# Ties at a row's threshold: kept by counting in the sorted list, instead of equality passes and a scan

## The chip, the cores and the metric

One core of a Trainium2 chip. The metric is device time in microseconds of one execution of the whole kernel, as the median of several runs. TensorE does the matmuls and transposes, VectorE and ScalarE the work on elements, GpSimd small powers; DMAs are issued by SyncE's queue (SP).

## The reference, cut to what matters

Four graph layers follow each other on `x` [2048, 128] with an adjacency of 2048 x 2048. The second one contains two attention steps with top-p sparsification, and the change lies there:

```python
probs = softmax(q @ k.T)                       # [2048, 2048]
idx = argsort(-probs)
sp = take_along_axis(probs, idx); cs = cumsum(sp)
keep_sorted = cs - sp < 0.9                    # TOP_P
mask = zeros.at[rows, idx].set(keep_sorted)
A = probs * mask
A = A / max(A.sum(-1), 1e-12);  Xa = A @ Xa    # twice, STEPS = 2
```

Per row the largest probabilities are kept until their sum reaches 0.9. The cut falls between two neighbours of the sorted row. If those two are equal (a tie), a comparison with the smallest kept value keeps both, and one of the equals has to be dropped: argsort is stable, so the first ones in the row are kept.

## The kernel before, in words

The 2048 rows are 16 tiles of 128. An attention step goes over four groups of four tiles (`G = 4`), so there are eight calls of `group(E, gi, left)`: `gi` 0 to 3 in the first step, 4 to 7 in the second; `left` counts the groups that still follow in the step (3 down to 0). `E` holds four tiles of unnormalised probabilities, 128 x 2048 float32 each, in `EA` for even and `EB` for odd groups.

VectorE works off its own instruction stream in program order. In a group it does the following.

1. `third_sum` and the steps before it guess a threshold `q.th` for each row, just above the true one.
2. `under` (L1934) writes the values under the guess into `cands[k]`; eight maxima of 8 values each per tile (L2071), then rounds of maximum and `match_replace` on 64 values (L2081, L2085) make `L`, the 32 largest values under the guess in sorted order. `crossing_checked` (L1954) scans `L` with the missing mass, adds 4.0 to the values behind the cut and takes the minimum: `s_(0)`, that is `s4[:, 0, :]`, the smallest kept value, a row's threshold. `after` is the largest value not kept.
3. `doubtful` (L2020) sets flags in `fl`: column 0 if anything is odd in any row, column `UNSURE` (4) if the list didn't reach the cut, columns `TIE + k` (8 to 11) if tile k has a row with `after >= s_(0)`. `any_row` (L1721) turns the 32 x 32 blocks of `fl` and reduces them, so that column 1 of `fl` holds each flag once for each block of 32 partitions.
4. With `left > 0`, first sums of the next group follow and the maximum of the one after next. `load_more()` (L1726) then loads flag 0 into four registers, one for each partition block, and adds them. With `left > 0` the masks are issued ahead of the branch: `masked` (L1967) writes `E * (E >= threshold)` to `cands[k]` with its sum in `Sk`.
5. `dve.If(more[0])`: the branch for odd groups. With `left == 0` it makes the masks there. It loads `UNSURE`; if that is set, `surely` (L2000) brackets and searches anew. Then `cut` (L1981) checks each tile's flag with `load_more(TIE + k)`, and for a tile with ties does an equality pass, a 2048-wide scan for the running sum of the tied values, three small steps, and two passes that subtract the surplus ones.
6. With `left == 0` the masks are made behind the branch (L2118 to L2121), each releasing TensorE by `mask_ok`; otherwise `kept_ok` (L2126, the reciprocal `rS`) releases it for the whole group.

`Steps` and `Dyn` count every VectorE instruction on a semaphore: `w(ins)` issues and waits for it, `w.put(ins)` only issues. `Dyn` counts from a register's value, for use inside branches, and `end` asserts its number of steps.

TensorE's order is written out by hand. `attend` (L746 on) transposes the kept rows (L527) and multiplies them (L778). For the last group of the second step (`gi == 7`) it comes behind `multiplied(3)` to `multiplied(11)` (L847), products of the third layer whose operands ScalarE finishes in L1267 and L1320. SP loads natural tiles of `adj` into `EA` behind `kept_ok` of group 6 and into `EB` behind that of group 7.

Of the kernel before, what the change touches and what calls it, by code (L numbers as in the profile page):

```python
# [7 lines left out]
ALU = mybir.AluOpType  # L8
# [6 lines left out]
P = 128  # L15
# [24 lines left out]
TOP = 8  # L40
# [54 lines left out]
def gnn_kernel(nc, x, adj, W0, b0, W1, W2, W3, U1, U2, ln_g, ln_b, L2W, L3W, b3, out):  # L95
# [18 lines left out]
    with ExitStack() as ctx:  # L114
        def sb(name, shape, dt=F32):
            return ctx.enter_context(nc.sbuf_tensor(name, shape, dt))
# [84 lines left out]
        fl = sb("fl", [P, 32], I32)  # L201
        ft = sb("ft", [P, 32], I32)
        ones = sb("ones", [P, WINDOW])
        Sk = sb("Sk", [P, G])
        rS = sb("rS", [P, 2, G])

# [1266 lines left out]
        def _(dve):  # L1473
# [3 lines left out]
            def tt(o, x0, x1, op):  # L1477
                return dve.tensor_tensor(o, x0, x1, op)
# [8 lines left out]
            def total(o, x0, op=ALU.add):  # L1487
                return dve.tensor_reduce(o, x0, AX.X, op)
# [17 lines left out]
            v.put(dve.memset(ones[:, :], 1.0))  # L1506
            v.put(dve.memset(below[:, :, :], 0.0))
            v(dve.memset(fl[:, :], 0))
            dve.wait_ge(in_x, 16)
            dve.wait_ge(expo_ok, 2)  # L1510
            sq_early = XT[:, BK:2 * BK].rearrange("p (k c) -> p k c", c=P)
# [214 lines left out]
            def load_more(c=0):  # L1726

                for m in range(4):
                    dve.reg_load(more[m], fl[32 * m + c:32 * m + c + 1, 1:2])
                for m in range(1, 4):  # L1730
                    dve.reg_add(more[0], more[0], more[m])

            def unfinished(w, window):

# [232 lines left out]
            def masked(w, E):  # L1967

                for k in range(G):
                    w.put(stt(cands[k], E[:, k, :], s4[:, 0, k:k + 1], ALU.is_ge, E[:, k, :], ALU.mult,  # L1970
                              accum_out=Sk[:, k:k + 1]))
# [9 lines left out]
            def cut(E, Tt, last):  # L1981


                for k in range(G):
                    load_more(TIE + k)
                    with dve.If(dve.snap(more[0])):
                        c = Dyn(sure_steps, sures, 8)
                        c(stt(tied, E[:, k, :], s4[:, 0, k:k + 1], ALU.is_equal, E[:, k, :], ALU.mult,
                              accum_out=Fv[:, k:k + 1]))
                        whole, spare = (E[:, k, :], cands[k]) if last else (cands[k], E[:, k, :])  # L1990
                        c.put(dve.tensor_tensor_scan(spare, tied, tied, 0.0, ALU.add, ALU.max))
                        c(tt(s4[:, 2, k:k + 1], Sk[:, k:k + 1], Tt[:, k:k + 1], ALU.subtract))
                        c(tt(s4[:, 2, k:k + 1], s4[:, 2, k:k + 1], Fv[:, k:k + 1], ALU.subtract))
                        c(tt(s4[:, 3, k:k + 1], s4[:, 0, k:k + 1], s4[:, 2, k:k + 1], ALU.subtract))
                        c(stt(tied, spare, s4[:, 3, k:k + 1], ALU.is_ge, tied, ALU.mult))
                        c(stt(whole, tied, -1.0, ALU.mult, whole, ALU.add, accum_out=Sk[:, k:k + 1]))
                        c.settle()
                        c.end()

            def surely(w, E, gi):  # L2000


                bracket(w, gi)
                unfinished(w, TOP)
                w.settle()
                more_rounds(E, gi, TOP)
                for k in range(G):
                    under(w, E, hi, k)
                w.wait()
                w.settle()  # L2010
                for k in range(G):
                    w.put(dve.max(V[:, k, :], cands[k]))
                w.wait()
                crossing(w, V, CU, TOP)
                masked(w, E)
                w.wait()
                ties(w)
                any_row(w)
# [15 lines left out]
            def group(E, gi, left):  # L2034


                q = guess_of[gi % 2]
                nq = guess_of[1 - gi % 2]

                def next_max(k):  # L2040
                    if left > 0:
                        row_max(gi + 1, k, k % 2)

                if gi in BOTH:
                    def early():
                        logit_mean(gi + 1)
                        next_max(0)

                    first_sums(E, gi, early)
                    third_sum(E, gi, lambda: next_max(1))  # L2050
                else:
                    third_sum(E, gi, lambda: next_max(1))

                for k in range(G):
                    if gi > 0:

                        dve.wait_ge(e_turned, 4 * (G * (gi - 1) + k + 1))
                    if gi not in BOTH and k == 0:
                        next_max(2)
                    under(v, E, q.th, k, accum_out=Lw[:, k:k + 1])  # L2060
                    v.wait()
                    if gi not in BOTH and k == 1:
                        next_max(3)
                    if k == G - 1:
                        v.put(tt(q.fval, q.spare, Lw[:, :], ALU.subtract))
                    for s in range(SETS):
                        if s == SETS // 2 and k < 2 and gi in BOTH:
                            next_max(k + 2)
                        if s == SETS // 2 and k == 2 and left > 0:
                            guess_gap(gi + 1)  # L2070
                        v.put(dve.max(tops[0][:, k, s * TOP:(s + 1) * TOP], cands[k][:, s * N // SETS:(s + 1) * N // SETS]))  # L2071
                    if k == 2 and left > 0:
                        guess_first(gi + 1)
                        dve.sem_inc(th_ok, 1)
                v.wait()
                v.put(total(seen8, tops[0][:, :, TOP - 1:SETS * TOP:TOP], ALU.max))
                for m in range(WINDOW // TOP):
                    if m > 0:

                        for k in range(G):  # L2080
                            v.put(dve.match_replace(tops[m % 2][:, k, :], L[:, k, (m - 1) * TOP:m * TOP],  # L2081
                                                    tops[(m - 1) % 2][:, k, :], 0.0))
                        v.wait()
                    for k in range(G):
                        v.put(dve.max(L[:, k, m * TOP:(m + 1) * TOP], tops[m % 2][:, k, :]))  # L2085
                    v.wait()
                if left > 1:
                    logit_mean(gi + 2)
                crossing_checked(q)
                doubtful()  # L2090
                if left > 0:
                    last_tile(nq, gi + 1)
                    surplus_below(nq, gi + 1, 0)
                    last_surplus(nq)
                    first_step(nq)
                    dve.sem_inc(th_ok, 1)
                    remember(nq, 0)
                if left > 1:
                    row_max(gi + 2, 0)
                load_more()  # L2100
                if left > 0:
                    masked(v, E)
                with dve.If(dve.snap(more[0])):
                    if left > 0:
                        v.wait()
                    else:
                        m = Dyn(sure_steps, sures, G)
                        masked(m, E)
                        m.wait()
                        m.end()  # L2110
                    load_more(UNSURE)
                    with dve.If(dve.snap(more[0])):
                        w = Dyn(sure_steps, sures, 52)
                        surely(w, E, gi)
                        w.settle()
                        w.end()
                    cut(E, q.Tt, left == 0)
                if left == 0:  # L2118
                    for k in range(G):
                        stt(cands[k], E[:, k, :], s4[:, 0, k:k + 1], ALU.is_ge, E[:, k, :], ALU.mult,  # L2120
                            accum_out=Sk[:, k:k + 1]).then_inc(mask_ok, 1)  # L2121
                    dve.wait_ge(mask_ok, G * (gi // NB + 1))
                else:
                    v.wait()
                v(ts(Sk[:, :], Sk[:, :], 1e-12, ALU.max))
                dve.reciprocal(rS[:, gi % 2, :], Sk[:, :]).then_inc(kept_ok, 1)  # L2126
                if left > 0:
                    v(tt(pa, soft, nq.inv_slope, ALU.mult))
                    v(tt(num, num, pa, ALU.add))
                    last_tile(nq, gi + 1)  # L2130
                    surplus_below(nq, gi + 1, 1)
                    last_surplus(nq)
                    next_step(nq, 0)
# [294 lines left out]
```

## Time and profile before

| | |
|---|---|
| median of 3 runs | 1088.53 us |
| lowest to highest | 1083.34 to 1089.64 us |
| the profiled execution: time | 1088.74 us |
| its span, first to last instruction | 1087.0 us |
| its mean granted TensorE clock | 0.854 of full |
| busy: PE, DVE, ACT, POOL | 75%, 75%, 47%, 6% |

The span is what the rows below count in; the 1.7 us between it and the execution's own time lie around it. PE is TensorE, DVE VectorE, ACT ScalarE, POOL GpSimd. A line such as L1485 is that of a helper (`stt`), so many different steps carry it; names and shapes tell them apart. An idle stretch "<-issue" is time in which the engine waited for nothing that the trace shows: its sequencer was busy with register loads, branches or fetching.

### The profile page before, as it was taken

The page shows a single profiled execution, that of the slowest core. Times are in us where ns is not written, and L with a number is a line of the kernel's source. Part 1 is how long each engine was busy: PE and PEld are TensorE (multiplying, and loading weights), DVE is VectorE, ACT ScalarE, POOL GpSimd, SP SyncE. Part 2 cuts the span into 40 slices and gives each one's busy share as a digit, 9 for nine tenths or more (in the row PEclk, how much of TensorE's full clock was granted, in tenths as well). Part 3 has the DMA queues.
Part 4 walks back from the last instruction along what each step waited for, and adds up shares of the span by engine and source line. Part 5 has one row for each costly group of instructions (what it writes and reads, how often), then busy time and mean ns, then how long its engine had stood idle before and what let it go on. Part 6 is the DMA issues. An engine that isn't in the chain of part 4 may idle for free. (4 is left out here: it accounts for less than half of the span.)

```text
span 1087.0 us, 12342 instructions
## 1 busy us (share of the span) xinstructions
PE 810.0 (75%) x3871; PEld 561.4 (52%) x3871; DVE 811.3 (75%) x2389; ACT 505.8 (47%) x973; POOL 70.5 (6%) x63
## 2 busy tenths in 40 slices
PE   5879968877886827376788787686088869997695
PEld 5744425555765717274565576573085456543342
DVE  5977769898999989933989898997789463235715
ACT  4867235366567475134526656748334122123212
POOL 0020000000000000000000000101001101002201
PEclk9989957888988868789796899898588989998798
DMA  9859203424013000000242402303141337600001
GB/s 342 337 190 432 75 9 146 150 83 156 1 45 112 1 2 1 0 2 0 78 155 82 151 1 75 135 1 126 39 163 39 117 120 296 281 1 0 1 0 39
DMA packets 20222, 108.25 MB, mean 100 GB/s; under 512 B 1825, under 2 KB 8753, under 8 KB 9777
## 3 DMA queue, kind: packets, MB, share of 16 engines
q1 hardware_dynamic: 18752, 106.77, 26.5%
q10 hardware_dynamic: 1392, 0.61, 0.2%
q8 instruction: 29, 0.48, 0.2%
q14 instruction: 49, 0.39, 0.1%
HBM read 88.23 MB, written 19.14 MB: 99 GB/s over the span
## 5 line engine op out<-in xcount | busy, mean ns | idle before, releaser
L1049 ACT ACTIVATE AT<-PS 128x512 f32<-128x512 f32 (+2 forms) x240 | 118.8, 553 | 167.3 <-PE PS L527 137.0
L527 PE MATMUL PS<-ident,AT 128*128 128x128 f32 x544 | 88.3, 300 | 110.2 <-DVE rS L2126 66.4
L527 PEld LDWEIGHTS PS<-ident,AT 128*128 128x128 f32 x544 | 70.8, 155 | 118.4 <-DVE rS L2126 69.0
L1485 DVE SCALAR_TENSOR_TENSOR AT<-EA,se 128x2048 uint8<-128x2048 f32 (+1 forms) x46 | 107.6, 2346 | 2.0 <-PE PS L527 0.7
L700 PE MATMUL PS<-K,ST 64*128 64x512 f32 x256 | 90.3, 802 | 22.6 <-ACT EA L1182 12.4
L1485 DVE SCALAR_TENSOR_TENSOR AT<-AT 128x2048 uint8<-128x2048 f32 (+2 forms) x50 | 100.7, 2013 | 1.1
L2071 DVE MAX8 AT<-AT 128x8 f32<-128x256 f32 x256 | 87.6, 412 | 0.7
L1624 DVE TENSOR_REDUCE mxv<-PS 128x1 f32<-128x2048 f32 x32 | 73.2, 2288 | 15.8 <-PE PS L700 15.4
L778 PE MATMUL PS<-hr,AT 128*128 128x128 f32 x512 | 71.7, 290 | 8.7 <-ACT AT L1049 7.8
L778 PE MATMUL PS<-AT 128*128 128x128 f32 x512 | 71.9, 290 | 7.7 <-ACT AT L1049 7.1
L778 PEld LDWEIGHTS PS<-hr,AT 128*128 128x128 f32 x512 | 65.2, 200 | 17.9 <-ACT AT L1049 11.9
L778 PEld LDWEIGHTS PS<-AT 128*128 128x128 f32 x512 | 65.4, 201 | 16.4 <-ACT AT L1049 11.8
L592 PE MATMUL PS<-AT 128*128 128x256 f32 x256 | 65.7, 415 | 10.5 <-DVE gs L1482 8.9
L592 PE MATMUL PS<-AT,hr 128*128 128x256 f32 x256 | 64.3, 408 | 11.8 <-DVE gs L1482 10.7
L1485 DVE SCALAR_TENSOR_TENSOR AT<-AT,s 128x2048 f32<-128x2048 f32 x22 | 50.6, 2349 | 24.5 <-issue 24.3
L592 PEld LDWEIGHTS PS<-AT 128*128 128x128 f32 x256 | 52.1, 209 | 25.2 <-DVE gs L1482 12.8
L592 PEld LDWEIGHTS PS<-AT,hr 128*128 128x128 f32 x256 | 51.1, 206 | 25.7 <-DVE gs L1482 14.2
L1049 ACT ACTIVATE ST<-PS 128x512 f32<-128x512 f32 (+2 forms) x35 | 19.2, 555 | 91.0 <-PE PS L1003 22.8
L700 PEld LDWEIGHTS PS<-K,ST 64*128 64x128 f32 x256 | 30.8, 240 | 57.4 <-issue 50.3
L651 PE MATMUL PS<-AT,R 128*128 128x512 f32 x128 | 58.4, 611 | 0.0
L1003 PE MATMUL PS<-AT,R 128*128 128x512 f32 x128 | 57.2, 592 | 0.0
L847 PE MATMUL PS<-AT,hr 128*128 128x512 f32 x96 | 48.7, 662 | 11.1 <-ACT hr L1320 11.1
(297 smaller groups left out, 1462.8 us busy)
## 6 DMA issues: line engine op xcount, KB each, us to landing
AT<-keep_at SPq DMA_DIRECT2D x32, 1024.0 KB, 5.1
EA<-in_adj SPq DMA_DIRECT2D x20, 1024.0 KB, 6.8
keep_at<-AT SPq DMA_DIRECT2D x8, 2048.0 KB, 24.9
AT<-keep_at SPq DMA_DIRECT2D x8, 2048.0 KB, 14.4
AT<-in_adj SPq DMA_DIRECT2D x12, 1024.0 KB, 4.9
EA<-keep_degrees SPq DMA_DIRECT2D x1, 1024.0 KB, 6.4
keep_x<-K SPq DMA_DIRECT2D x4, 256.0 KB, 6.9
out<-EA SPq DMA_DIRECT2D x4, 256.0 KB, 2.3
```

Source lines behind the costliest of these rows:

```text
L527: return pe.transpose(dst, src, ident[0:p, 0:p])
L592: mm = pe.matmul(bank(6)[:, 2 * P:4 * P], left[:, j, :], slab[:, j, :], start=(j == 0), stop=(j == NT - 1))
L651: mm = pe.matmul(halves(4 + b % 2), R[:, j, :], AT[:, 2 * b:2 * b + 2, j, :], start=(j == 0), stop=(j == NT - 1))
L700: return pe.matmul(bank(to + n), ST[1][half_rows, k * P:(k + 1) * P], keys[half_rows, n * BK:(n + 1) * BK], start=True, stop=True)
L778: mm = pe.matmul(bank(6)[:, 0:P], stg[b % 2][:, n * P:(n + 1) * P], left[:, j, :], start=(j == 0), stop=(j == NT - 1))
L847: mm = pe.matmul(bank(n), hr[:, t, :], natural(t)[:, n * BK:(n + 1) * BK], start=(t == 0), stop=(t == NT - 1))
L1003: mm = pe.matmul(halves(4 + i % 2), R[:, j, :], AT[:, 2 * b:2 * b + 2, j, :], start=(j == 0), stop=(j == NT - 1))
L1049: return act.activation(dst, src, ACT.Copy)
L1485: return dve.scalar_tensor_tensor(out=o, in0=x0, scalar=s, in1=x1, op0=op0, op1=op1, **k)
L1624: v(dve.tensor_reduce(mxv[:, odd:odd + 1], PS[:, b:b + 4, :], AX.XY, ALU.max))
L2071: v.put(dve.max(tops[0][:, k, s * TOP:(s + 1) * TOP], cands[k][:, s * N // SETS:(s + 1) * N // SETS]))
```

## The change

A row of counts 1 to 8 (`counted`) is made once at the start. In the branch, `tied_counted` counts for each row how often the threshold occurs among the kept values of the sorted list `L`, and makes `V`: the threshold that many times, then zeros. More than 8 occurrences make the row unsure. `joined` brings each flag of the four partition blocks into one, so that a flag is one register load (`load_joined`) in place of four and three adds. For a tile with ties `first_tied` lets `match_replace` put 4.0 in the place of the first occurrences of the values in `V`, and one pass keeps what is greater than the threshold. With `left == 0` the masks inside the branch are gone. `surely` and `cut` stay for unsure groups; `first_tied` stands in the Else part.

```diff
--- before.py
+++ after.py
@@ -201,6 +201,8 @@
         fl = sb("fl", [P, 32], I32)
         ft = sb("ft", [P, 32], I32)
         ones = sb("ones", [P, WINDOW])
+        counted = sb("counted", [P, TOP])
+        flags = sb("flags", [P, 4], I32)
         Sk = sb("Sk", [P, G])
         rS = sb("rS", [P, 2, G])
 
@@ -1506,6 +1508,7 @@
             v.put(dve.memset(ones[:, :], 1.0))
             v.put(dve.memset(below[:, :, :], 0.0))
             v(dve.memset(fl[:, :], 0))
+            v(dve.tensor_tensor_scan(counted[:, :], ones[:, 0:TOP], ones[:, 0:TOP], 0.0, ALU.mult, ALU.add))
             dve.wait_ge(in_x, 16)
             dve.wait_ge(expo_ok, 2)
             sq_early = XT[:, BK:2 * BK].rearrange("p (k c) -> p k c", c=P)
@@ -1729,6 +1732,17 @@
                     dve.reg_load(more[m], fl[32 * m + c:32 * m + c + 1, 1:2])
                 for m in range(1, 4):
                     dve.reg_add(more[0], more[0], more[m])
+
+            def joined(w):
+
+                for m in range(4):
+                    w.put(dve.tensor_copy(flags[0:32, m:m + 1], fl[32 * m:32 * (m + 1), 1:2]))
+                w.wait()
+                w(dve.tensor_reduce(ft[0:32, 0:1], flags[0:32, :], AX.X, ALU.max))
+
+            def load_joined(c):
+
+                dve.reg_load(more[0], ft[c:c + 1, 0:1])
 
             def unfinished(w, window):
 
@@ -1994,6 +2008,31 @@
                         c(tt(s4[:, 3, k:k + 1], s4[:, 0, k:k + 1], s4[:, 2, k:k + 1], ALU.subtract))
                         c(stt(tied, spare, s4[:, 3, k:k + 1], ALU.is_ge, tied, ALU.mult))
                         c(stt(whole, tied, -1.0, ALU.mult, whole, ALU.add, accum_out=Sk[:, k:k + 1]))
+                        c.settle()
+                        c.end()
+
+            def tied_counted(w):
+
+                w(tt(LS[:, :, :], L[:, :, :], s4[:, 0, :].unsqueeze(2).to_broadcast([P, G, WINDOW]), ALU.is_equal))
+                w(total(s_(2), LS[:, :, :]))
+                w.put(tt(V[:, :, :], counted[:, :].unsqueeze(1).to_broadcast([P, G, TOP]),
+                         s4[:, 2, :].unsqueeze(2).to_broadcast([P, G, TOP]), ALU.is_le))
+                w(ts(s_(5), s_(2), TOP + 0.5, ALU.is_gt))
+                w.put(tt(V[:, :, :], V[:, :, :], s4[:, 0, :].unsqueeze(2).to_broadcast([P, G, TOP]), ALU.mult))
+                w(tt(s_(5), s_(5), s_(3), ALU.max))
+                w(dve.tensor_reduce(fl[:, UNSURE:UNSURE + 1], s_(5), AX.X, ALU.max))
+                any_row(w)
+                joined(w)
+
+            def first_tied(E, last):
+
+                for k in range(G):
+                    load_joined(TIE + k)
+                    with dve.If(dve.snap(more[0])):
+                        c = Dyn(sure_steps, sures, 3)
+                        c(dve.match_replace(tied, V[:, k, :], E[:, k, :], 4.0))
+                        c(stt(E[:, k, :] if last else cands[k], tied, s4[:, 0, k:k + 1], ALU.is_gt, E[:, k, :], ALU.mult,
+                              accum_out=Sk[:, k:k + 1]))
                         c.settle()
                         c.end()
 
@@ -2103,18 +2142,18 @@
                 with dve.If(dve.snap(more[0])):
                     if left > 0:
                         v.wait()
-                    else:
-                        m = Dyn(sure_steps, sures, G)
-                        masked(m, E)
-                        m.wait()
-                        m.end()
-                    load_more(UNSURE)
+                    t = Dyn(sure_steps, sures, 14)
+                    tied_counted(t)
+                    t.end()
+                    load_joined(UNSURE)
                     with dve.If(dve.snap(more[0])):
                         w = Dyn(sure_steps, sures, 52)
                         surely(w, E, gi)
                         w.settle()
                         w.end()
-                    cut(E, q.Tt, left == 0)
+                        cut(E, q.Tt, left == 0)
+                    with dve.Else():
+                        first_tied(E, left == 0)
                 if left == 0:
                     for k in range(G):
                         stt(cands[k], E[:, k, :], s4[:, 0, k:k + 1], ALU.is_ge, E[:, k, :], ALU.mult,
```

## Rows read from the trace of the kernel before

**Rows 1.** Page, part 1: busy us of each engine (share), instructions

```profile
PE 810.0 (75%) x3871; PEld 561.4 (52%) x3871; DVE 811.3 (75%) x2389; ACT 505.8 (47%) x973; POOL 70.5 (6%) x63
```

**Rows 2.** VectorE's timeline in group 6: start us, us, what, [idle before, releaser]

```profile
759.40 2.35 DVE L1485 SCALAR_TENSOR_TENSOR AT<-EA,s 128x2048 f32<-128x2048 f32 x1 [1.73 <-issue]
...
773.22 2.35 DVE L1485 SCALAR_TENSOR_TENSOR AT<-EA,s 128x2048 f32<-128x2048 f32 x1 [4.64 <-issue]
...
775.61 4.42 DVE L1991 TENSOR_TENSOR_SCAN EA<-AT 128x2048 f32<-128x2048 f32 x1
...
792.18 0.17 DVE L1482 TENSOR_SCALAR Sk<-Sk 128x4 f32<-128x4 f32 x1 [6.99 <-issue]
```

**Rows 3.** VectorE's timeline in group 7

```profile
842.75 2.35 DVE L1485 SCALAR_TENSOR_TENSOR AT<-AT,s 128x2048 f32<-128x2048 f32 x1 [2.15 <-issue]
...
865.62 2.35 DVE L1485 SCALAR_TENSOR_TENSOR AT<-AT,s 128x2048 f32<-128x2048 f32 x1 [13.70 <-issue]
...
868.01 4.42 DVE L1991 TENSOR_TENSOR_SCAN AT<-AT 128x2048 f32<-128x2048 f32 x1
...
877.74 2.35 DVE L1485 SCALAR_TENSOR_TENSOR AT<-AT,s 128x2048 f32<-128x2048 f32 x1
```

**Rows 4.** TensorE's waits, 740 to 890: us in total, times, longest

```profile
PE PS L527 <- DVE rS L2126: 32.6, 1, 32.6
...
PE PS L527 <- DVE AT L1485: 9.6, 1, 9.6
```

**Rows 5.** TensorE's timeline, 792 to 896

```profile
792.62 1.97 PE L527 MATMUL PS<-ident,AT 128*128 128x128 f32 x8 [32.64 <-DVE rS L2126]
...
854.88 12.20 PE L847 MATMUL PS<-EA,hr 128*128 128x512 f32 x24 [3.16 <-ACT hr L1320]
866.92 3.60 PE L847 MATMUL PS<-AT,hr 128*128 128x512 f32 x8
880.15 1.97 PE L527 MATMUL PS<-ident,AT 128*128 128x128 f32 x8 [9.64 <-DVE AT L1485]
...
889.14 0.27 PE L527 MATMUL PS<-ident,T 128*128 128x128 f32 x1
...
895.70 0.27 PE L527 MATMUL PS<-ident,T 128*128 128x128 f32 x1
```

**Rows 6.** VectorE's small steps before the branch of group 6

```profile
746.61 0.29 DVE L1478 TENSOR_TENSOR AT<-AT 128x124 f32<-128x124 f32 x1
...
748.84 0.16 DVE L2031 TENSOR_REDUCE fl<-s 128x1 int32<-128x4 f32 x1
749.03 0.21 DVE L1723 STREAM_TRANSPOSE ft<-fl 128x32 int32<-128x32 int32 x1
749.28 0.19 DVE L1724 TENSOR_REDUCE fl<-ft 128x1 int32<-128x32 int32 x1
```

**Rows 7.** VectorE's timeline in group 3, branch not taken

```profile
465.89 2.35 DVE L1485 SCALAR_TENSOR_TENSOR AT<-AT,s 128x2048 f32<-128x2048 f32 x1 [4.84 <-issue]
```

**Rows 8.** VectorE by line and shape: count, busy us, mean ns, idle before

```profile
L2071 DVE MAX8 AT<-AT 128x8 f32<-128x256 f32 x256 | 87.6, 412 | 0.7
...
L2085 DVE MAX8 AT<-AT 128x8 f32<-128x64 f32 x128 | 19.3, 213 | 0.8
L2081 DVE MATCH_REPLACE8 AT<-AT 128x64 f32<-128x64 f32 x96 | 19.0, 209 | 0.0
...
L2081 DVE MATCH_VALUE_LOAD AT<-AT 128x8 f32 x96 | 8.1, 84 | 0.8
```

**Rows 9.** Stretches: length, busy us of PE, PEld, DVE, ACT, POOL, clock, DMA share, GB/s

```profile
880.00:889.00 9.00, 8.85 (x55) 8.61 (x56) 7.89 (x11) 2.85 (x6) 0.00 (x0) 0.69 0.12 15
889.00:896.00 7.00, 6.83 (x59) 6.35 (x57) 0.00 (x0) 3.62 (x10) 0.00 (x0) 1.00 0.97 404
```

**Rows 10.** VectorE at the start

```profile
11.49 2.29 DVE L1488 TENSOR_REDUCE nd<-EA 128x1 f32<-128x2048 f32 x1 [10.44 <-DMA K<-in_x]
```

## The prediction

> **What bounds the kernel now.** I read the page's busy shares first [rows 1]. TensorE and VectorE are each busy three quarters of the span, so no engine's total settles anything. What counts is who waits at the place the diff touches. The diff works inside one branch of `group`, so the second view is VectorE's timeline, to see in which of the eight groups (two steps of four) that branch runs. The 2048-wide scan of line 1991 stands there twice, in groups 6 and 7 counting from 0 [rows 2, 3]. No instruction of lines 2007 to 2018 (`surely`) is in the trace. So the branch runs in the last two groups, each time for ties in one tile, and the expensive search never. The reader should see there the three passes over 2048 values and, larger, the holes marked "issue": VectorE idles 4.64 and 6.99 us around group 6's tie pass and 13.70 us before group 7's [rows 2, 3]. In them its sequencer loads flags into registers and branches.
>
> Third, TensorE's waits between 740 and 890 us [rows 4]: 32.6 us for `rS`, the last thing group 6 makes, and 9.6 us for a row mask of group 7. So both tails release TensorE. TensorE's timeline [rows 5] gives the important detail. After group 6 is released at 792.62 it has its own work until 870.52 (the last batch starts at 866.92 and lasts 3.60), and only then waits, until 880.15. What group 7 saves beyond those 9.64 us relative to TensorE is worth nothing.
>
> **What goes, what comes.** In group 6 the tail runs from the end of the masks, 773.22 - 4.64 = 768.58, to 792.18: 23.60 us. It is 4.64 idle, 11.97 of passes and small steps (773.22 to 785.19), 6.99 idle [rows 2]. The last hole is three checks of later tiles that turn out false, 2.33 each; the first is two checks, 2.32 each. Each check is four register loads, three adds, a branch and the skip. The four loads and adds alone, ahead of the masks, leave a hole of 1.73 [rows 2], so branch and skip are 0.60.
>
> The new tail, added up:
> - `tied_counted`, 14 steps: two over 128 values at 0.29 plus some 0.03 between [rows 6]; transpose and reduction of the flags 0.45; the others small, 0.19 apart when they wait [rows 6], about 0.1 when they don't. 0.64 + 0.45 + five waited at 0.2 + two put and four copies at 0.08 to 0.1 = 2.6 us; 3.0 if the copies between partition blocks hold each other up.
> - Five checks with one load in place of four. If the four loads share 1.73 evenly, one is 0.43 and a check 1.03. If the 1.73 is one latency that four overlapping loads share, a check stays at 2.33. Neither row decides; I take 0.7 for the load, nearer to the even share because the adds also belong to the 1.73, so 1.3 a check, 6.5 us.
> - The way to the Else part skips `surely` and all four bodies of `cut`. For a long skip the trace has two answers: group 3, whose branch is not taken, leaves 4.84 us before its masks, group 7, whose branch is taken, 2.15 [rows 3, 7], so the skip of the whole body costs 2.69; while skipping `surely` alone in group 6 costs no more than a short one (two checks in 4.64). The new skip is nearly the whole body: I take 2.7, bound 0.
> - The tie pass of one tile: value load 0.08, replacement over 2048, product 2.35. Replacement is seen only over 64 values, 209 ns; the maximum instruction gives a slope, (412 - 213) / 192 = 1.04 ns a value [rows 8], so 209 + 1984 x 1.04 = 2.27 us; upper bound the scan's 4.42 [rows 2]. With gaps 4.8 us, bound 7.0. I take the slope: both instructions cost the same at 64.
>
> Sum 2.6 + 6.5 + 2.7 + 4.8 = 16.6 us against 23.60: group 6 saves 7.0 us (bounds: 12.6 new, saves 11.0; 24.4 new, loses 0.8). TensorE starts right behind `rS` [rows 5], and its work up to 870.52 hangs on it, directly or through ScalarE and GpSimd steps that it feeds, so I move all of it by the full saving. The natural tiles that SP loads when group 6 reports (and, later, those of group 7) are issued earlier by as much. VectorE's group 7 moves as well; it has no hole before 842.75 but the 2.15 of its loads and branch.
>
> In group 7 the tail runs from 842.75 to 877.74, where the final masks start: 34.99 us [rows 3]. It holds four masks whose result only `cut` used; they go to the unsure branch, where they don't run. The new tail is again 16.6, so the masks come 18.4 us earlier; even at the upper bound of 24.4 they come 10.6 earlier. Either way TensorE's wait of 9.64 goes entirely, and what is late next is TensorE's own work before it. Group 7 gives 9.6 us, whatever the unknown prices.
>
> A second gain follows. After the wait TensorE's granted clock is at the low level: 0.69 of full in 880 to 889, 1.00 in 889 to 896 [rows 9]. The first tile takes 880.15 to 889.14 = 8.99 us, the second, with no less work, 6.56 [rows 5]. Without the idle stretch the last batch before it, and so the first tile too, run at 2.4 GHz: 2.4 us more.
>
> Costed at nothing: the scan of `ones` into `counted` lies in VectorE's wait of 10.44 us for the first input [rows 10]; were it exposed it would be some 0.2 us. In the six groups without ties the branch only skips a longer body; in five of them behind four masks of 2.3 us each, as today, and in group 3 exposed, with 2.7 us already paid. The new waits are all VectorE on its own steps; behind them stand the final masks and `rS`, for which TensorE waits, and they are in the 2.6.
>
> **Two rules of the Trainium skill beside the rows.** The Trainium skill, DMA: Bandwidth & Descriptors (Latency and other measured facts), gives a register load a floor of about 600 ns and says that the compiler unrolls four of them to spread it. That speaks against this change, which replaces four loads by a lone one: an estimate by that page is 1.2 us a check and a gain of 19.5 in all; no run here shows one load alone. Its page Runtime: NRT & Kernel Launch (Instruction fetch mechanics) says that a taken branch to outside the fetched window stalls for a fetch. Group 3 agrees (4.84 against 2.15), group 6's skip does not show it; by the rule the skip costs its 2.7, without it the whole gain would be 21.7.
>
> **The sum.** 7.0 + 9.6 + 2.4 = 19.0 us. The profiled execution took 1088.74, span 1087.0; the median is 0.2 below, so 1088.53 - 19.0 = 1069.5. The three runs spread over 6 us, and about 1% is what a measurement of this kernel can tell from no change.
>
> **The rivals.**
> - Checks cost by latency, not by count: 2.33 each, so group 6 saves 7.0 - 5.2 = 1.8, or loses 0.8 if replacement also goes at the scan's rate. With 12.0 from group 7 the gain is 11 to 14 us: 1074.5 to 1077.5. For it: nothing in the trace separates the loads. Chance 0.20.
> - Everything cheap: checks 1.03, no stall at the skip. Group 6 saves 11, together 23: 1065.5. Chance 0.08.
> - Group 7's gain is lost: some other input of TensorE's work after 870.52 is late, or its earlier work doesn't move with the release. Only group 6's 7 us stay: 1081.5. Against it: TensorE's waits between 740 and 890 that name a step of another engine name steps fed by TensorE itself, but for these two. Chance 0.07.
> - Slower: the count makes rows unsure that were not. It decides when some row holds nine or more kept values equal to its threshold (above TOP + 0.5). Then `surely` runs: four `under` passes and four masks and four tie passes at 2.35, four 2048-wide maxima at 412 + 1792 x 1.04 = 2.27 us, together 37 us, and some 10 of loads, checks and small steps, without a single round of search; `cut` stays on top. One group so hit gives about 1135, two 1180. For it only that a threshold of many equal values is conceivable; against it, only one tile of each group has ties. This is also the case that the change doesn't do what it says. Chance 0.05.
> - The forecast, gain 16 to 22 with the tie pass or a check off by a little: 0.60.
>
> 1064 to 1078 takes in the forecast, both cases of the check's price and their bounds, and leaves out the last two rivals, 0.12, and some spread. Faster by over 1% (10.9 us): forecast, the cheap case and nearly all of the first rival, 0.85. Within 1%: its edge and the lost gain, 0.10. Slower 0.05.
>
> **What the new profile would show.** No scan on 2048 values, a replacement of about 2.3 us in groups 6 and 7; holes of about 1.3 us per check in place of 2.33 (the first rival says 2.3); one hole of some 4 us before the tie pass; no wait of TensorE between its last batch and the first transposes of group 7, and that tile in 6.6 us at full clock; TensorE's wait for group 6's `rS` about 7 us shorter. Wrong would be: any instruction of `surely`, TensorE waiting for something new ahead of group 7, or a replacement near 4 us.

## The result, and the profile after

| | before | after |
|---|---|---|
| median | 1088.76 us (4 runs, 1083.34 to 1089.64) | 1060.60 us (4 runs, 1059.20 to 1062.30) |
| profiled execution, span | 1088.74, 1087.0 us | 1062.30, 1060.5 us |

The ratio is 0.9756, with a 95% interval from 0.9726 to 0.9785: some 26.6 us faster (23 to 30) where 19.0 was forecast, and below the range, which ended at 1064. A second measurement on another chip gave 0.9757 (0.9732 to 0.9783). The two profiled executions differ by 26.5 us in span; that is the difference to account for.

VectorE's timeline in group 6 of the changed kernel answers to [rows 2] (helpers have moved by two lines):

```profile
758.53 2.35 DVE L1487 SCALAR_TENSOR_TENSOR AT<-EA,s 128x2048 f32<-128x2048 f32 x1 [1.75 <-issue]
...
767.83 0.29 DVE L1480 TENSOR_TENSOR AT<-AT,s 128x128 f32<-128x128 f32 x1
...
770.43 0.14 DVE L1741 TENSOR_REDUCE ft<-flags 32x1 int32<-32x4 int32 x1
774.70 0.09 DVE L2033 MATCH_VALUE_LOAD AT<-AT,EA 128x8 f32 x1 [4.12 <-issue]
774.78 2.28 DVE L2033 MATCH_REPLACE8 AT<-AT,EA 128x2048 f32<-128x2048 f32 x1
777.09 2.35 DVE L1487 SCALAR_TENSOR_TENSOR AT<-AT,s,EA 128x2048 f32<-128x2048 f32 x1
...
781.90 0.17 DVE L1484 TENSOR_SCALAR Sk<-Sk 128x4 f32<-128x4 f32 x1 [2.45 <-issue]
```

The masks end at 767.71. Counting, flags and joining take 2.86 us to 770.57. Then come 4.12 us for two checks and the skip to the Else part, 4.75 us of tie pass, and 2.45 us for the three checks that turn out false, 0.82 each where they were 2.33. The replacement over 2048 values takes 2.28 us (2.27 forecast). From the masks' start to the sum's step it is 23.37 us, and was 32.78: the tail is 9.4 us shorter.

Group 7 answers to [rows 3]:

```profile
832.27 0.29 DVE L1480 TENSOR_TENSOR AT<-AT,s 128x128 f32<-128x128 f32 x1 [1.94 <-issue]
...
845.76 0.09 DVE L2033 MATCH_VALUE_LOAD AT<-AT 128x8 f32 x1 [10.73 <-issue]
...
850.65 2.35 DVE L1487 SCALAR_TENSOR_TENSOR AT<-AT,s 128x2048 f32<-128x2048 f32 x1
```

One hole of 10.73 us stands between joining and the tie pass: the tie is in the last of the four tiles here (no hole for a further check follows the tie pass), so all five checks and the skip lie in it. From the branch's first step to the final masks it is 18.4 us, and was 35.0.

TensorE's timeline answers to [rows 5], its waits between 720 and 900 us to [rows 4]:

```profile
782.34 1.97 PE L529 MATMUL PS<-ident,AT 128*128 128x128 f32 x8 [23.30 <-DVE rS L2165]
...
837.39 13.90 PE L849 MATMUL PS<-EA,hr 128*128 128x512 f32 x32
851.12 3.60 PE L849 MATMUL PS<-AT,hr 128*128 128x512 f32 x8
854.56 1.04 PE L529 MATMUL PS<-ident,AT 128*128 128x128 f32 x8
...
861.32 0.27 PE L529 MATMUL PS<-ident,T 128*128 128x128 f32 x1
```

```profile
PE PS L529 <- DVE rS L2165: 23.3, 1, 23.3
PE PS L849 <- ACT hr L1322: 11.6, 2, 7.8
```

The wait for group 7's mask is gone: the first transposes start at 854.56, right behind the last batch, and the first mask was done at 853.0. The first tile takes 6.76 us and not 8.99. The granted clock in these stretches, for [rows 9]:

```profile
852.00:861.00 9.00, 8.75 (x61) 7.03 (x60) 8.80 (x11) 2.63 (x5) 0.00 (x0) 1.00 0.00 0
861.00:868.00 7.00, 6.86 (x61) 6.54 (x59) 0.00 (x0) 3.55 (x10) 0.00 (x0) 1.00 0.95 366
```

But there is something that the forecast doesn't have. From the release by `rS` to the start of the last batch of 8 matmuls it was 866.92 - 792.62 = 74.30 us; now it is 851.12 - 782.34 = 68.78. Where TensorE waited 3.16 us for ScalarE's L1320 and then ran 24 matmuls in 12.20 us, it now runs 32 in one piece of 13.90. What ScalarE waits for there are three small steps of GpSimd. Its timeline before:

```profile
847.60 2.10 POOL L462 TENSOR_SCALAR nd<-nd 128x4 f32<-128x4 f32 x1 [16.21 <-ACT hr L1267]
849.78 3.00 POOL L464 TENSOR_TENSOR es<-nd,ex 128x4 f32<-128x4 f32 x1
852.86 0.20 POOL L466 TENSOR_TENSOR ri<-Dn,es 128x4 f32<-128x4 f32 x1
```

and after:

```profile
836.86 0.19 POOL L464 TENSOR_SCALAR nd<-nd 128x4 f32<-128x4 f32 x1 [15.74 <-ACT hr L1269]
837.25 1.01 POOL L466 TENSOR_TENSOR es<-nd,ex 128x4 f32<-128x4 f32 x1 [0.20 <-POOL nd L464]
838.34 0.20 POOL L468 TENSOR_TENSOR ri<-Dn,es 128x4 f32<-128x4 f32 x1
```

From first start to last end that is 5.46 us before and 1.68 after, for the same 4 values a partition. Before, VectorE ran group 7's masks at that time (842.75 to 851.91); now it stands in its hole of 10.73 us. The last two of these masks:

```profile
847.30 2.35 DVE L1485 SCALAR_TENSOR_TENSOR AT<-AT,s 128x2048 f32<-128x2048 f32 x1
...
849.57 2.34 DVE L1485 SCALAR_TENSOR_TENSOR AT<-AT,s 128x2048 f32<-128x2048 f32 x1
```

GpSimd's first step begins under the pass that ends at 849.65 and ends at 849.70; the power step begins under the pass that ends at 851.91 and ends 0.87 us after it; the third begins when VectorE is free and takes its 0.20. So a step that began under such a pass ended only behind it, by 0.05 us for the short steps and by some 0.87 us for the power step.

So the 26.5 us of span are: 0.9 before the masks of group 6; 9.4 in its tail; 5.5 from release to last batch; 9.8 from there to the first transposes; 2.2 in the first tile; and 1.3 given back behind it. The last part lies in one batch of 64 matmuls behind a wait, 29.20 us before and 30.75 after; it is not of the change, since a second execution of the changed kernel took 29.17 us for it. Of the 5.5 us, 5.1 lie between the start of the first eight of these 32 matmuls (848.13 before, 837.39 after) and the last batch: 18.79 and 13.73 us. The rest is an earlier batch of eight behind another wait for ScalarE, 6.74 and 6.27 us.

Group 3, whose branch is not taken, is as before [rows 7]:

```profile
464.97 2.35 DVE L1487 SCALAR_TENSOR_TENSOR AT<-AT,s 128x2048 f32<-128x2048 f32 x1 [4.76 <-issue]
```

### The profile page after: what moved, and what is told of

Read it like the earlier page. It is cut to its first block and busy times, and to the rows that moved or that the text cites. A ratio compares the mean times of both kernels' runs of the same rounds, so it can differ in the third digit from the quotient of the medians.

```text
span 1060.5 us, 12334 instructions
## 1 busy us (share of the span) xinstructions
PE 808.1 (76%) x3871; PEld 560.2 (53%) x3871; DVE 792.9 (75%) x2400; ACT 506.1 (48%) x973; POOL 67.0 (6%) x63
## 5 line engine op out<-in xcount | busy, mean ns | idle before, releaser
L1487 DVE SCALAR_TENSOR_TENSOR AT<-AT 128x2048 uint8<-128x2048 f32 (+2 forms) x48 | 96.1, 2002 | 1.1
L780 PEld LDWEIGHTS PS<-AT 128*128 128x128 f32 x512 | 63.9, 197 | 16.6 <-ACT AT L1051 12.1
L1184 ACT ACTIVATE AT<-PS,negmax 128x2048 f32<-128x2048 f32 x16 | 31.5, 1966 | 48.9 <-DVE negmax L1484 48.9
```

The lines of the kernel that those rows point to most:

```text
L780: mm = pe.matmul(bank(6)[:, 0:P], stg[b % 2][:, n * P:(n + 1) * P], left[:, j, :], start=(j == 0), stop=(j == NT - 1))
L1487: return dve.scalar_tensor_tensor(out=o, in0=x0, scalar=s, in1=x1, op0=op0, op1=op1, **k)
```

## The experiments

A kernel is compared with the kernel before on the same chip; "above" and "below" between two changed kernels is taken from the ratios where they ran apart. Where the edit lies behind that point, the profiled executions reach the masks of group 6 anywhere from 755 to 759 us, so the spans themselves are no better than some 3 us, and the stretches between two events of one trace say more.

### GpSimd under VectorE's passes

Two kernels fill the hole in group 7 of the changed kernel with four passes over 2048 values. The tie pass comes 0.8 us later for it, counted from the branch's first step (14.24 and 14.30 us, 13.49 in the changed kernel). In the first kernel the passes read two SBUF tensors, in the second one.

```diff
-                    t = Dyn(sure_steps, sures, 14)
+                    t = Dyn(sure_steps, sures, 14 if left > 0 else 14 + G)
                     tied_counted(t)
+                    if left == 0:
+                        masked(t, E)
```

```diff
+                    if left == 0:
+                        for k in range(G):
+                            t.put(total(Fv[:, k:k + 1], E[:, k, :], ALU.max))
```

> The changed kernel with four more 2048-wide passes with two SBUF inputs (the masks that the change took out of the branch) issued on VectorE in group 7 right behind the counting, without a wait, so that they fill VectorE's hole of 10.7 us while its sequencer loads flags. Their result is overwritten; the output stays the reference's. Theory A (GpSimd's three small steps for ScalarE's L1322 are held up by such passes; they took 5.46 us under them before and 1.68 us without after): GpSimd takes 5 to 6 us again, TensorE waits some 3 us ahead of its x32 batch and runs part of it at the lower clock, its last batch ends about 5 us later, and the time is 4 to 6 us above the changed kernel. Theory B (TensorE's shorter chain has another cause): no change within 1 us, GpSimd's three steps stay near 1.7 us.

> As the run with two inputs, but the four passes are maxima over 2048 values with one SBUF input and one value out, 2.29 us each by the rows of the same shape. Output unchanged. Theory A in its narrow form (only passes that read two SBUF tensors hold GpSimd up): GpSimd's three steps take about 1.7 us and the time is that of the changed kernel within 1 us. If any busy VectorE does it: 4 to 6 us more, as with two inputs. Theory B: no change.

With two inputs the ratio is 0.9833 (0.9805 to 0.9861), median 1066.03; with one 0.9765 (0.9730 to 0.9800), median 1058.47, on the same chip. GpSimd's timeline with two inputs:

```profile
836.56 1.52 POOL L464 TENSOR_SCALAR nd<-nd 128x4 f32<-128x4 f32 x1 [14.83 <-ACT hr L1269]
838.16 3.00 POOL L466 TENSOR_TENSOR es<-nd,ex 128x4 f32<-128x4 f32 x1
841.24 1.39 POOL L468 TENSOR_TENSOR ri<-Dn,es 128x4 f32<-128x4 f32 x1
```

with one:

```profile
833.27 0.19 POOL L464 TENSOR_SCALAR nd<-nd 128x4 f32<-128x4 f32 x1 [15.93 <-ACT hr L1269]
833.67 1.01 POOL L466 TENSOR_TENSOR es<-nd,ex 128x4 f32<-128x4 f32 x1 [0.20 <-POOL nd L464]
834.75 0.20 POOL L468 TENSOR_TENSOR ri<-Dn,es 128x4 f32<-128x4 f32 x1
```

6.07 us against 1.68. TensorE's timeline with two inputs, then with one:

```profile
782.95 1.97 PE L529 MATMUL PS<-ident,AT 128*128 128x128 f32 x8 [24.77 <-DVE rS L2167]
...
844.45 10.54 PE L849 MATMUL PS<-EA,hr 128*128 128x512 f32 x24 [3.76 <-ACT hr L1322]
854.83 3.60 PE L849 MATMUL PS<-AT,hr 128*128 128x512 f32 x8
```

```profile
778.57 1.97 PE L529 MATMUL PS<-ident,AT 128*128 128x128 f32 x8 [22.91 <-DVE rS L2168]
...
833.81 13.90 PE L849 MATMUL PS<-EA,hr 128*128 128x512 f32 x32
847.54 3.60 PE L849 MATMUL PS<-AT,hr 128*128 128x512 f32 x8
```

With two inputs TensorE waits 3.76 us ahead of the batch, with one it runs 32 matmuls in one piece as in the changed kernel. So these passes do hold GpSimd up, and the one-input passes don't: the narrow form of theory A stands, theory B falls. Here too each step ends right behind the pass under which it began: VectorE's passes end at 838.02, 840.30 and 842.57, the steps at 838.08, 841.16 and 842.63. Two things differ between the two kinds of pass, though: the one-input passes also write one value a partition and the others 2048, and no run here separates inputs from output width. Two kernels of the next section agree: the kernel before with joined flags, which keeps the four masks, has 1.94 and 3.00 us for the first two steps; the changed kernel with four loads, which has no such passes there, has 0.19 and 1.01.

From release to last batch it is 71.88 us with two inputs and 68.97 with one. That understates the effect, because an earlier batch of eight took 5.37 and 6.47 us. From the first eight matmuls (837.09 and 833.81) to the last batch it is 17.74 and 13.73: 4.0 us, where the kernel before has 5.1. It is less than in the kernel before because the clock did not fall in this wait (24 matmuls in 10.54 us at a granted clock of 1.00; in the kernel before 12.20 us at 0.86). The medians lie 7.6 us apart, more than that and more than the 4 to 6 expected; of the 7.7 us between the spans 2.6 lie before group 6's masks and 1.8 in group 6's tail, where this build's first hole is 5.89 us in place of 4.12. Why that hole grew is open.

The converse, on the kernel before: the four masks inside the branch left out.

```diff
                     else:
-                        m = Dyn(sure_steps, sures, G)
-                        masked(m, E)
-                        m.wait()
-                        m.end()
+                        pass
```

> The kernel before without the four masks inside the branch of groups 3 and 7 (group 3 doesn't take it). The sum that cut takes for the surplus in group 7 is then that of an earlier group, so which of the tied values are dropped there is not the reference's; the number and size of all passes stay. The masks take 9.2 us of VectorE. Theory A: the final masks come 9.2 us earlier, GpSimd's three steps fall to about 1.7 us, TensorE's own work ends about 5 us earlier, and it waits 5 to 6 us, not 9.6, for the first mask: the time is 9.2 us below before, bound by VectorE. Theory B (no effect on GpSimd): TensorE's own work ends where it did, so its wait falls to 0.5 us and the clock does not drop: 9 to 11 us below before.

Ratio 0.9913 (0.9883 to 0.9943), 9.5 us below before, as both theories had it, since VectorE sets the release. GpSimd's and TensorE's timelines tell them apart:

```profile
843.34 1.01 POOL L464 TENSOR_TENSOR es<-nd,ex 128x4 f32<-128x4 f32 x1 [0.20 <-POOL nd L462]
```

```profile
789.43 1.97 PE L527 MATMUL PS<-ident,AT 128*128 128x128 f32 x8 [34.12 <-DVE rS L2123]
...
843.48 13.90 PE L847 MATMUL PS<-EA,hr 128*128 128x512 f32 x32
857.21 3.60 PE L847 MATMUL PS<-AT,hr 128*128 128x512 f32 x8
867.30 1.97 PE L527 MATMUL PS<-ident,AT 128*128 128x128 f32 x8 [6.49 <-DVE AT L1485]
```

The power step takes 1.01 us in place of 3.00, TensorE's stretch is 67.78 us in place of 74.30, and it waits 6.49 us for the mask: theory A. Of the 6.5 us, 5.1 lie between the first eight matmuls and the last batch (13.73 us as in the changed kernel); the rest is the earlier batch of eight, 5.29 us in place of 6.74, which ends before the masks would begin.

### The price of a check

The changed kernel with four loads for each flag, and the kernel before with joined flags alone:

```diff
             def load_joined(c):
-                dve.reg_load(more[0], ft[c:c + 1, 0:1])
+                load_more(c)
```

```diff
-                    load_more(UNSURE)
+                    t = Dyn(sure_steps, sures, 5)
+                    joined(t)
+                    t.end()
+                    load_joined(UNSURE)
...
-                    load_more(TIE + k)
+                    load_joined(TIE + k)
```

> The changed kernel with each single flag load replaced by the four loads and three adds of before; all else stays. Loads cost by count (0.50 us for each load with its add, from checks of 2.33 before and 0.82 after): checks of 2.33 again, group 6's tail 7.5 us longer (14.2 to 21.7), group 7's hole 10.7 to 18.2, so TensorE waits there some 6 us and restarts at the lower clock for 2 us more: 15 us above the changed kernel. If one latency were shared by overlapping loads the checks would stay near 0.8 and nothing would change.

> The kernel before with one part of the change alone: flags of the four partition blocks joined by five small steps at the head of the branch, and one load in place of four in each of the five checks. Equality passes, scan and the masks in group 7 stay. By count of loads: each check 1.5 us shorter, five checks 7.5, less 0.9 for the joining, so 6.6 us in group 6 and, since TensorE's wait of 9.64 in group 7 is longer than that, 6.6 there too: 13 us below before. If group 7's share were lost: 6.6. If loads overlapped: slower by 1 to 2.

With four loads the ratio is 0.9876 (0.9828 to 0.9923), 13 us above the changed kernel (15 expected). Its five runs spread widely, from 1066.65 to 1077.87 us, so the size is known to some 5 us only; the stretches within the trace are firmer. VectorE in group 6 and TensorE's wait in group 7:

```profile
778.38 0.09 DVE L2033 MATCH_VALUE_LOAD AT<-AT,EA 128x8 f32 x1 [6.94 <-issue]
...
790.17 0.17 DVE L1484 TENSOR_SCALAR Sk<-Sk 128x4 f32<-128x4 f32 x1 [7.04 <-issue]
```

```profile
868.49 1.97 PE L529 MATMUL PS<-ident,AT 128*128 128x128 f32 x8 [6.41 <-DVE AT L1487]
```

Three checks take 7.04 us, 2.35 each, against 0.82 in the changed kernel: (2.35 - 0.82) / 3 = 0.51 us for one load with its add. So loads cost by count. TensorE waits 6.41 us again and restarts at the low clock (1.97 us for the first transposes).

Joined flags alone in the kernel before give 0.9889 (0.9860 to 0.9918), 12.1 us below before (13 expected). VectorE in group 6:

```profile
769.16 0.14 DVE L1739 TENSOR_REDUCE ft<-flags 32x1 int32<-32x4 int32 x1
771.20 2.35 DVE L1486 SCALAR_TENSOR_TENSOR AT<-EA,s 128x2048 f32<-128x2048 f32 x1 [1.90 <-issue]
...
785.25 0.17 DVE L1483 TENSOR_SCALAR Sk<-Sk 128x4 f32<-128x4 f32 x1 [2.07 <-issue]
```

Two checks with one load take 1.90 us, three 2.07. The joined flags pay in both groups, because TensorE's wait of 9.64 in group 7 falls to 3.62:

```profile
867.03 1.09 PE L528 MATMUL PS<-ident,AT 128*128 128x128 f32 x8 [3.62 <-DVE AT L1486]
```

### The long skip

The changed kernel without the search and `cut` in the unsure branch; no row needs them with these inputs.

```diff
                     with dve.If(dve.snap(more[0])):
-                        w = Dyn(sure_steps, sures, 52)
-                        surely(w, E, gi)
+                        w = Dyn(sure_steps, sures, 1)
                         w.settle()
                         w.end()
-                        cut(E, q.Tt, left == 0)
```

> The changed kernel with the search for unsure rows and cut left out of all eight groups (a settle in their place); no row needs them with these inputs, so the output is unchanged. This shortens the code that is skipped. Theory A (a skip over a long body costs a fetch of 2.5 us): group 6's hole of 4.12 us becomes 1.6 to 1.7, group 3's hole of 4.76 us before its masks 2.1 to 2.3, group 7's 10.7 some 4 to 5 but behind TensorE's own work; in all about 5 us below the changed kernel. Theory B (the holes are register work of the branch, not fetches): holes and time unchanged.

Ratio 0.9706 (0.9685 to 0.9727), 5.4 us below the changed kernel. VectorE before the masks of group 3, and before the tie pass of group 6:

```profile
464.13 2.35 DVE L1487 SCALAR_TENSOR_TENSOR AT<-AT,s 128x2048 f32<-128x2048 f32 x1 [2.53 <-issue]
```

```profile
769.75 0.09 DVE L2033 MATCH_VALUE_LOAD AT<-AT,EA 128x8 f32 x1 [1.55 <-issue]
```

The holes fall from 4.76 to 2.53 and from 4.12 to 1.55 us: the long skip costs 2.2 to 2.6 us there, two short checks take 1.55. In group 7 the hole falls from 10.73 to 3.35, by 7.4 us, nearly three times as much; which of the skips between its five checks pay is open. The rule of the Trainium skill, Runtime: NRT & Kernel Launch (Instruction fetch mechanics), of a stall for a branch out of the fetched window agrees. But no such stall shows at one of the long skips: in the kernel before with joined flags the first two checks of group 6, one of which skips `surely`, take 1.90 us together.

### Better versions

First the loads of flag 0, moved behind the issue of a 2048-wide pass in the six groups with a follower:

```diff
             def last_tile(q, gi, under_it=None):
                 mass_above(EA if gi % 2 == 0 else EB, gi, G - 1)
+                if under_it is not None:
+                    under_it()
                 v.wait()
...
-                    last_tile(nq, gi + 1)
+                    last_tile(nq, gi + 1, load_more)
...
-                load_more()
                 if left > 0:
                     masked(v, E)
+                else:
+                    load_more()
```

> The changed kernel with the four loads of flag 0 moved, in the six groups that are followed by another, from right before the masks to right behind the issue of the 2048-wide pass of the next group's last tile. The loads then run while VectorE works on that pass of 2.35 us, and the hole of 1.75 to 1.85 us ahead of the masks goes. Output unchanged. If VectorE's chain sets the time of these groups: 6 x 1.8 = 10.8 us below the changed kernel. If TensorE or ScalarE set it in some groups, those give less: at least group 6 (1.8), where TensorE waits 23 us for rS. My value: 7 to 11 us below.

Ratio 0.9719 (0.9691 to 0.9746), and on another chip 0.9679 (0.9654 to 0.9704), medians 1054.16 and 1053.36: 4 to 8 us below the changed kernel, where 7 to 11 was expected. The hole ahead of the masks is gone in all six groups; in group 6:

```profile
750.05 0.16 DVE L1866 COPY se<-AT 128x4 f32<-128x4 f32 x1
750.12 2.35 DVE L1487 SCALAR_TENSOR_TENSOR AT<-EA,s 128x2048 f32<-128x2048 f32 x1
```

Six holes of 1.8 would be 10.8 us. The masks of group 6 start 8.4 us earlier than in the changed kernel (6.4 against its second execution), so some groups give less. The starts of the masks show which: from group 1 to 2 it is 1.4 us shorter (74.49 us in the changed kernel, 73.14 and 73.03 in the two executions here), from 3 to 4 it is 2.2 shorter (137.31; 135.13 and 135.09), from 0 to 1, 2 to 3 and 4 to 5 it stays within 0.5 us; from 5 to 6 it varies by more than that from one execution to the next (78.6 to 80.2). What limits those groups instead was not tested.

Then the branches turned round as well, with masks or sums and the reciprocal inside the case that occurs (`If(more[0] < 1)`: `kept()`, Else: the rest), so that the long skip comes last.

> The kernel with the early flag loads, and in addition the branches turned round: the case that occurs (no ties; ties but no unsure row) comes first, with the group's final masks or sums and the reciprocal inside it, and the sequencer skips the search only after it has issued them. Output unchanged. Theory A (the long skip costs 2.2 to 2.6 us, as the run without the search showed in groups 3 and 6): group 3's hole before its masks 2.1 to 2.3 in place of 4.85, group 6's first hole 1.6 in place of 4.1, group 7's shorter but behind TensorE: 4 to 5 us below the kernel with the early loads, 10 to 12 below the changed kernel. If the fetch comes back at some other branch: no gain over the early loads.

This was a miss. Ratio 0.9813 (0.9787 to 0.9838), median 1066.38, where the changed kernel on the same chip had 1059.17. VectorE in groups 0, 5 and 3:

```profile
260.60 0.16 DVE L1480 TENSOR_TENSOR se<-se,AT 128x4 f32<-128x4 f32 x1 [4.43 <-issue]
...
696.21 0.36 DVE L1480 TENSOR_TENSOR se<-se 128x4 f32<-128x4 f32 x2 [5.42 <-issue]
```

```profile
464.68 2.35 DVE L1487 SCALAR_TENSOR_TENSOR AT<-AT,s 128x2048 f32<-128x2048 f32 x1 [2.09 <-issue]
```

Group 3 does what was expected, 2.09 us, and so does group 6's first hole, 1.42. But in all six groups with a follower (0 to 2 and 4 to 6) the skip now stands behind the reciprocal, where no pass covers it: holes of 4.43, 3.29, 2.61, 3.00, 5.42 and 3.19 us, 21.9 in all. In the changed kernel it runs under the masks. The changed kernel beside it:

> The changed kernel itself, on the same chip as the one with the branches turned round, as the measure for it. 1057 to 1063 us; the GpSimd steps of 1.7 us, the holes of 4.1 and 2.4 us in group 6 and 4.8 in group 3 as before.

Ratio 0.9757 (0.9732 to 0.9783), holes as expected. So turning round only groups 3 and 7:

> The kernel with the early flag loads, and the branches turned round in groups 3 and 7 alone: there the final masks stand inside the case that occurs and the long skip comes behind their issue, while they run. In the other six groups, where turning round put the skip behind rS and delayed the next group's work by 2.6 to 4.4 us each, the order stays that of the kernel with the early loads. Output unchanged. Expected: group 3's hole 2.1 in place of 4.85, no hole behind rS in groups 0 to 2 and 4 to 6, 2 to 3 us below the kernel with the early loads. If the skip behind the masks of group 3 delays the second step instead: no gain.

> The kernel with the early flag loads once more, on the same chip as the one with the branches turned round in groups 3 and 7, as the measure for it: 1052 to 1056 us.

```profile
460.08 2.35 DVE L1487 SCALAR_TENSOR_TENSOR AT<-AT,s 128x2048 f32<-128x2048 f32 x1 [2.10 <-issue]
```

Group 3's hole is 2.10 us in place of 4.78, and no hole stands behind `rS`. Ratio 0.9668 (0.9643 to 0.9693), median 1051.38, against 0.9679 and 1053.36 for the early loads alone: 1 to 2 us below where 2 to 3 was expected, and the intervals overlap, so that the time alone does not tell the two apart; the hole does. Group 7's hole before the tie pass is 3.60 us here, which TensorE's own work covers. It has the lowest median here, 36 us below before.

## Why the prediction was right or wrong

- Where the branch runs, and that both tails release TensorE: right.
- Group 7 gives the whole of TensorE's wait: right (9.8 for 9.6), but by less than it seemed. The forecast had 18.4 - 9.6 = 8.8 us to spare; the first mask was ready 1.6 us before TensorE was free. TensorE came 5.5 us earlier than forecast, and group 7's tail was 18.4 us in place of 16.6. The tail was taken as equal to group 6's, but its hole of 10.73 us is 3.9 more than five checks of 0.82 and a skip of 2.7. That such an error did not reach the time is luck.
- The restart at the low clock: right, 2.2 for 2.4.
- The tie pass: right, 4.75 for 4.8; the replacement by the slope of the maxima 2.28 for 2.27. The 14 steps took 2.86 for 2.6.
- The long skip: right in size in group 6, whose hole is 2.6 us shorter without the search and `cut`; wrong in group 7, where it is 7.4, off TensorE's path.
- The check was mis-sized: 1.3 us forecast, 0.82 measured. Five of them are the 2.4 us that group 6 saved beyond the 7.0. I had named 1.03 as the low end, by splitting the 2.33 into 0.60 for branch and skip and 1.73 for loads; the run with four loads gives 0.51 for each load with its add, which leaves 0.3 for branch and skip if a lone load costs as much. The rival in which a check costs by latency fell, and with it the estimate of 1.2 us from the Trainium skill's page DMA: Bandwidth & Descriptors.
- The step that failed is "its work up to 870.52 hangs on it, directly or through ScalarE and GpSimd steps that it feeds, so I move all of it by the full saving". It took TensorE's stretch as rigid, and it costed the masks taken out of group 7's branch as VectorE's time alone. They also held up GpSimd's steps on the way to ScalarE's L1320. With them gone the stretch is 5.5 us shorter: about 3.3 are the wait, 1.7 the clock that fell in it (24 matmuls in 12.20 us, 10.54 at the full clock), and 0.5 an earlier batch, which ran before the masks began. This is shown from both sides: taking the masks from the kernel before brings GpSimd to its short times and the stretch to 67.8 us; putting two-input passes into the changed kernel brings back 6.07 us for GpSimd's steps and a wait of 3.76 for TensorE; one-input passes don't. The Trainium skill, GPSIMD Engine Reference (Specifications), says that GpSimd shares its SBUF interfaces with VectorE and contends with VectorE instructions of two SBUF inputs; the runs agree, and it is the rule that I should have weighed. The runs alone don't separate the number of inputs from the width of what is written.

The two errors, 2.4 and 5.5, with 0.9 ahead of group 6 (of the kind by which executions differ anyway) and 1.3 given back, are the 7.5 us between 19.0 and 26.5.

## What to carry to other kernels

When a pass is removed, look at every engine that worked while it ran: a small GpSimd step that begins under a long two-input VectorE pass ends only behind that pass, and a chain behind those steps shortens when they go, even where VectorE's own time is covered. In data-dependent branches count the register loads (0.5 us each here) and the long skips (2.2 to 2.6 us in two places, 7.4 in a third), and issue a long pass ahead of both; a skip placed behind the last issued instruction is paid in full.

## What the runs showed of the hardware

- GpSimd's steps on 4 values a partition: 5.46 to 6.07 us for three of them under two-input passes of VectorE (float32, 2048 wide), 1.68 us under one-input passes or none. Each slowed step ended 0.05 to 0.06 us (the power step 0.86 to 0.87) behind the pass under which it began.
- Behind a wait of 3.16 us TensorE ran 24 matmuls in 12.20 us in one kernel, at a granted clock of 0.86 over that stretch; behind a wait of 3.76 us in another the same 24 took 10.54 us at 1.00. No run here shows why.
- `match_replace` over 2048 float32 values takes 2.28 us, as a one-input reduction does.
- A flag load into VectorE's sequencer costs 0.51 us with its add, as the difference between checks of four loads and of one shows, and loads in a row add up.
